# A routed feed-forward kernel on one core: the table places of a batch are worked out one slot earlier, and spread and published at the front of the next

## The reference, cut to what matters

```
x = x + softmax(layernorm(x) @ ctx.T * scale + mask) @ ctx      # per batch
n = layernorm(x);  probs = softmax(n @ gate_weight.T)
top_val, top_idx = top_k(probs, 8); top_val /= top_val.sum()
# experts chosen only as 5th to 8th may be remapped to a similar primary one,
# decided over ALL tokens
out = x + sum over the 8 experts of top_val * (silu(gate) * up) @ down
```

## Time and profile before

| | us |
|---|---|
| median of 3 runs (804.34 to 804.52) | 804.4 |
| the profiled execution, its own time | 807.05 |
| its span, first to last instruction | 805.3 |

### The profile page before, as it was taken

One profiled execution on the slowest core, in us unless ns is written; L12 is line 12 of the kernel. 1 busy time (PEld: TensorE's weight loads), 2 busy tenths in 40 slices (PEclk: granted clock), 3 DMA queues, 4 the chain that ended last, 5 costly groups with the idle time before them and its releaser, 6 DMA issues. The chain is left out here.

```text
span 805.3 us, 15215 instructions
## 1 busy us (share of the span) xinstructions
PE 676.6 (84%) x4278; PEld 560.5 (70%) x4278; DVE 541.6 (67%) x1213; ACT 450.7 (56%) x891; POOL 516.2 (64%) x461
## 2 busy tenths in 40 slices
PE   4999999630599999999998998999988998989730
PEld 2555565320589999888988888878877977878630
DVE  5699898861276667776677777776767777767611
ACT  3444454310366666666775766757666676666610
POOL 6037777776738877887766666676657666666421
PEclk9999999855599999999999999999999999999965
DMA  8999999505659999999999999999999999999576
GB/s 304 349 313 332 322 330 301 170 12 159 177 154 220 244 240 237 239 247 255 247 268 256 268 241 259 245 245 258 236 260 217 250 236 245 233 246 232 107 132 152
DMA packets 107557, 189.93 MB, mean 236 GB/s; under 512 B 33521, under 2 KB 35441, under 8 KB 106065
## 3 DMA queue, kind: packets, MB, share of 16 engines
q1 hardware_dynamic: 74274, 125.61, 50.2%
q0 software_dynamic: 33200, 63.35, 38.9%
HBM read 143.40 MB, written 56.24 MB: 248 GB/s over the span
## 5 line engine op out<-in xcount | busy, mean ns | idle before, releaser
L1223 PE MATMUL bank<-xh,w1h 128*128 128x256 f32 (+7 forms) x768 | 229.3, 299 | 21.4 <-DVE h L887 21.2
L1224 PE MATMUL bank<-xl,w1h 128*128 128x256 f32 (+7 forms) x768 | 220.5, 287 | 0.0
L1225 PE MATMUL bank<-xh,w1l 128*128 128x256 f32 (+7 forms) x768 | 220.4, 287 | 0.0
L608 POOL DMA_INDIRECT xg<-normed_tokens,list x145 | 159.3, 1099 | 62.5 <-issue 55.9
L1223 PEld LDWEIGHTS bank<-xh,w1h 128*128 128x128 f32 x768 | 147.5, 192 | 27.0 <-issue 26.7
L617 POOL DMA_INDIRECT out_rows<-ys,list x73 | 116.7, 1599 | 72.9 <-ACT ys L1040 60.4
L903 DVE TENSOR_TENSOR xl<-bank,xh 128x448 fp32r<-128x448 f32 (+3 forms) x145 | 84.3, 616 | 115.1 <-ACT xh L1047 115.0
L592 POOL DMA_INDIRECT list_table<-token,slot x112 | 112.4, 1004 | 69.7 <-ACT token L1001 35.9
L617 POOL DMA_INDIRECT second_sum<-ys,list x70 | 111.2, 1589 | 64.5 <-ACT ys L1040 43.5
L1224 PEld LDWEIGHTS bank<-xl,w1h 128*128 128x128 f32 x768 | 147.9, 193 | 0.1
L1225 PEld LDWEIGHTS bank<-xh,w1l 128*128 128x128 f32 x768 | 147.6, 192 | 0.0
(11 more groups left out here) (204 smaller groups left out, 1084.7 us busy)
## 6 DMA issues: line engine op xcount, KB each, us to landing
raw<-in_w SPq DMA_DIRECT2D x195, 256.0 KB, 4.7
raw<-in_w2a SPq DMA_DIRECT2D x65, 256.0 KB, 5.0
ctxT_s<-in_ctxT SPq DMA_DIRECT2D x16, 768.0 KB, 7.3
ctx_s<-in_ctx SPq DMA_DIRECT2D x16, 768.0 KB, 8.8
raw<-in_w2b SPq DMA_DIRECT2D x65, 128.0 KB, 5.9
list_table<-blank SPq DMA_DIRECT2D x30, 256.0 KB, 7.6
x_in<-in_x SPq DMA_DIRECT2D x16, 224.0 KB, 4.5
out_rows<-x SPq DMA_DIRECT2D x16, 224.0 KB, 8.8
```

The source lines that it names most:

```text
L608: pool.indirect_dma_start(xg[u.on(XGS)][0:u.m, t, :], None, normed, bass.IndirectOffsetOnAxis(ap=lists[u.on(LISTS)][0:u.m, t, 0:1], axis=0 ...
L1223: pe.matmul(bank[m][:, 0:W], wh, mh, start=(c == 0), stop=False)
L1224: pe.matmul(bank[m][:, 0:W], wh, ml, start=False, stop=False)
L1225: mm = pe.matmul(bank[m][:, 0:W], wl, mh, start=False, stop=(c == DK - 1))
```

## The change

The arithmetic stays. What moves, in slot s:

- TensorE: `spread` (s-4) goes from the end to second place, between `turn_probs` and `scores`. `turn_xn2` (s-2) and `places` (s-3) follow `scores` directly; `readout`, `logits` and `turn_xn` come after them.
- VectorE: `place_entries` leaves the front of the slot. It now handles batch s-3, of the same slot's `top`, after `score`: its first five instructions alone (`AHEAD = 5`), the other six by turns with `resid`. `count_tokens` (s-4) comes before `score`.
- ScalarE: `publish` (s-4) goes from last place to a place right after the `rough` step of `scales`.
- The plan's chains run in slot `TOTALS_AT` itself, with `place_entries` of the last batch.

```diff
@@ VectorE @@
             def slot(s):
                 Chain.start_again(dve)
-                if s.n == TOTALS_AT + 1:
-                    dve.wait_ge(plan_ps, 1)
-                    turns(place_entries(s - 4), replaceable(), ranks(), remap())
-                else:
-                    going = [scales(s)]
-                    batches(s, (4, lambda b: going.append(place_entries(b))), (3, lambda b: going.append(top(b))),
-                            (-2, lambda b: going.append(norm(b))))
-                    turns(*going)
+                going = [scales(s)]
+                batches(s, (3, lambda b: going.append(top(b))), (-2, lambda b: going.append(norm(b))))
+                turns(*going)
+                taking_turns(s, (4, count_tokens))
                 taking_turns(s, (0, score))
                 if s.n == 0:
                     constants()
-                taking_turns(s, (1, resid))
-                taking_turns(s, (4, count_tokens))
+                if s.n == TOTALS_AT:
+                    dve.wait_ge(plan_ps, 1)
+                    turns(place_entries(s - 3), replaceable(), ranks(), remap())
+                else:
+                    going = []
+                    batches(s, (3, lambda b: going.append(place_entries(b))))
+                    for chain in going:
+                        for _ in range(AHEAD):
+                            next(chain)
+                    batches(s, (1, lambda b: going.append(resid(b))))
+                    turns(*going)
@@ ScalarE @@
-                batches(s, (2, norm_x1), (3, exps), (-1, norm_x), (2, copy_xn2T), (0, exp_scores), (-1, copy_xnT), (4, publish))
+                batches(s, (4, publish), (2, norm_x1), (3, exps), (-1, norm_x), (2, copy_xn2T), (0, exp_scores), (-1, copy_xnT))
@@ TensorE @@
-                batches(s, (1, turn_probs), (0, scores), (1, readout), (2, turn_xn2), (-1, turn_xn), (2, logits), (3, places))
+                batches(s, (1, turn_probs), (4, spread), (0, scores), (2, turn_xn2), (3, places))
                 if s.n == TOTALS_AT:
                     totals()
-                batches(s, (4, spread))
+                batches(s, (1, readout), (2, logits), (-1, turn_xn))
@@ constants @@
 TOTALS_AT = B + 2
+AHEAD = 5
```

## The result

| | before | after |
|---|---|---|
| median, us | 804.5 | 816.8 (815.05 to 818.95, 4 runs) |
| profiled execution, us | 807.05 | 816.61 |
| its span | 805.3 | 814.8 |
| first entry, last entry | 50.67, 196.01 | 45.35, 205.85 |
| first lists loaded | 198.94 | 210.34 |

The changed kernel is slower: ratio 1.015, interval 1.0134 to 1.0166, or +12.4 us against a forecast of +0.9. The whole loss is there when stage 2 begins (+11.4 at the first gather); from the gather to the end the two profiled executions need 603.6 and 601.7 us. In the changed kernel the lines of TensorE stand 5 further on: `spread` L1157 and L1158, `scores` L1120, `turn_xn2` L1108, `places` L1146 to L1148, `readout` L1129, `logits` L1137; `norm_x1` is L979, `publish` L1005 and L1006.

A forecast was written before the change was run, and what follows sets the result against it. GpSimd's entry stream bounded the kernel before; the new order's 9.5 us ring would make it wait. The stream ending 0.8 us earlier plus one clock fall of 1.7 gave +0.9, a median of 805.3 us, range 801.0 to 808.8.

The forecast's parts named there:

- What bounds the kernel before: Stage 1: ends by GpSimd's stream of 112 entries, 9.11 us a batch, against TensorE's slot of 8.72 us.
- The start of the stream: Slots 2 and 3: `place_entries` of batch 0 starts at 37.05, the first entry at 46.1, 4.5 us earlier.
- The chain on VectorE: `place_entries` in two pieces, five instructions alone, six by turns with `resid`: 5.15 us, bounds 5.0 and 5.3.
- The ring: `place_entries`, `spread`, `scores`, `turn_xn2`, `places` and back to `place_entries` with handoffs: 9.49, say 9.5 us a slot.
- the other ways round: Other dependency paths in a slot, claimed shorter than the 9.5 us ring; `scales` to `place_entries` 9.0 us.
- The clock: TensorE's granted clock at `scores`: one fall to 1.2 GHz taken, costing 1.7 us of the end.
- clock falls again and again: Rival, `scores` on TensorE: 1.7 us per fall, 807.0 us at two, 808.7 at three; chance 0.28.
- The sum: Stage 1: 3.7 of 4.5 us given back over 12 slots, batch 13 at 168.7 to 168.8, stream ends 0.8 us earlier.
- The plan: Before stage 2: plan some 5 us later, weights land about 197, lists wait for entries until 198 anyway.
- the rival of 0.03: The plan is late, before stage 2: 805.3 us and 1 more; chance 0.03.
- The third rival, GpSimd stays the bound: VectorE's chain 0.4 us or more shorter, slot below 9.11, full 4.5 us stay: 799.9 us; chance 0.12.

The follow-up runs named there:

- experiment 5: Changed kernel with `spread` behind `scores` and `publish` behind `norm_x1` and `exps`: 802.0 us; its last run, also with `turn_xn` ahead of `logits`: 801.7 us.
- experiment 1: Changed kernel with two matmuls of no use per slot (the filler) in TensorE's idle before `spread`: 810.3 us, ratio 1.0058 to the kernel before.
- Experiments 2 and 3: Changed kernel with `spread` behind `scores` (2: 812.7 us, ratio 1.0094); with AHEAD = 11, all of `place_entries` before `resid` (3: 817.9 us, 1.0155).
- experiment 4: Changed kernel with `publish` alone moved behind `norm_x1` and `exps` on ScalarE: 820.8 us, ratio 1.0189 to the kernel before.
- kernel before with six entries: Kernel before with six of seven table entries issued per batch, on a slow chip: 823.0 us, ratio 0.9762; a first time 821.6 us, 0.9761.
- filled kernel: Changed kernel with two useless matmuls per slot in TensorE's idle before `spread`, on a slow chip: 843.1 us, ratio 1.0014 to the kernel before.

## Why the prediction was wrong

*What bounds the kernel before.* Right: the stream's start and its rate; experiment 5 gains what an earlier start of an unbroken stream gives.

*The start of the stream.* Right: forecast 46.1, measured 45.35; first `place_entries` 36.70 against 37.05.

*The chain on VectorE.* Right to the hundredth: 5.15.

*The ring.* It exists as described and binds, TensorE idle 1.23 us before `spread` by L742. Two terms were too short by 0.1 each. `spread` and `turn_xn2` were taken at 0.44 and 0.39 from the earlier trace rows, where transposes of the same kind follow them; here `scores` and `places` follow, each of which begins with matmuls of bf16, and they take 0.54 and 0.49. `turn_probs` shows the same: 0.29 from its start to the next where the filler, f32, follows it (97.98, 98.27 in experiment 1), 0.39 where `scores` follow it (102.60, 102.99 in the last run of experiment 5). Over 12 slots 2.3 us, as the prediction had said of such an error. I had said that the other ways round are shorter and stopped there; for `scales` to `place_entries` I had 9.0. Experiments 2 and 3 show the two next ones at 9.9 and 10.2 as soon as the order is touched, so "the ring is 9.5, GpSimd 9.11" left no room for a repair of one edge.

*The clock.* **This step failed.** "The kernel before has one in some ten slots. I take one." I carried a rate over from a kernel without the idle into one with 1.2 us of it in every slot, though the same passage had idle making falls likelier. The runs showed four in the ring, 1.68 us each (11.36 against 9.68), so three more than taken, 5.0 us, and one behind the ring (there the kernel before is at the lower clock too, 0.50 from 165 to 175 us, with nothing waiting on it). The Trainium skill (TensorE: Matmul & The Clock Gate, Part 1: The HAM clock gate) has the gate follow how busy TensorE has been; experiment 1 agrees, four falls in the ring to none with the idle filled; experiments 2 and 3, as idle and without a fall, show that the amount of idle alone does not tell. The rival "clock falls again and again" was the true one, at 0.28, but counted to three only: at four falls it gives 810.4.

*The sum.* Batch 13 was to start at 168.8, with the one fall 170.5; it started at 179.33. Of the 8.8 us, 5.0 are the falls, 2.3 the ring, less 0.4 of the earlier start, and the rest, 1.9, falls to the two slots behind the ring, in which `readout` at the lower clock takes 4.52 us (169.10) for 2.81.

*The plan.* "The lists wait for the entries until 198 anyway" looked at the weights' end by itself. The plan came 16 us later, not 5 (L742 of the last batch 192.17, before 175.98), and its weights lay over the last entries and made them land 1.5 us later. That was the rival of 0.03 with its price of 1 us. 8.8 and 1.5 are 10.3, and with the +0.9 forecast that is the +11.4 at the first gather but for 0.2. The other microsecond of the +12.4 is not placed. The prediction took the profiled execution to stay 2.65 over the median; it was 0.2 under it (816.61, 816.83), and the two profiled executions differ by 9.6 alone.

*The third rival, GpSimd stays the bound.* Refuted: the chain took 5.15 us, as counted from the earlier trace rows with each start 0.04 us behind an end, and the ring 9.68. The rival would have held had the ring been shorter by 0.6. The Trainium skill (VectorE: DVE Perf Modes, The DRAIN you can't avoid) has eight copies as fast with a semaphore after each as without; nothing here shows such a gain for this chain.

## What to carry to other kernels

Moving a step to the front of a slot can close a ring through work that it didn't depend on before: write down every ring of the new order with its length, the second and third too, since opening one brings up the next. An idle stretch of TensorE on the ring costs its own length and may cost the clock of what stands behind it; if the new order has idle in each slot, take falls as repeated, and price them on the ring. Slots only 0.4 us longer than the engine that sets the rate needs give back an earlier start of 5 us in a dozen slots.

## What was not expected of the hardware

- The falls came with great regularity, at 42.69, 73.52, 104.24 and 135.04 us, each third slot, and with `publish` moved on another engine (experiment 4) at 51.96, 83.22, 114.46, 127.04 and 158.06, with one gap of a single slot. The kernels with as much idle in two pieces (experiments 2 and 3) had none. Which property of the idle decides was not separated.
- The same kernel takes 804 to 806 us on some chips and 842 on two others. An entry costs GpSimd the same 1.26 us on both kinds; on the slow ones what waits for `spread` starts 2.4 us (kernel before with six entries) or 3.2 us (filled kernel) behind its end, 0.04 in the kernel before on the first chip. The late lists there (214.90 in the kernel before with six entries, whose last entry starts at 202.95) don't show a late landing: SyncE issues the weights first, up to 213.96, and the lists come 0.94 us behind them.
